# A deformable-patch tokenizer in a vision tower: the four images of a sampling step moved from 32-row bands to 80 adjacent partitions, their places loaded by one transfer

## The reference, cut to what matters

```python
off = conv(x, offset_w, stride 16)            # 2 x 256 offsets (dy, dx) for each of the 800 patches
py  = base_y + ki + dy ;  px = base_x + kj + dx     # 256 places in each patch
sampled = bilinear(x, py, px)                 # zero outside the image
out = einsum('bhwkc,ock->bohw', sampled, Wk)  # 192 x 768, then norm, GELU
```

## Time and profile before

| | us |
|---|---|
| median of 3 runs | 1366.1 |
| lowest, highest | 1360.94, 1372.89 |
| profiled execution, whole run | 1369.17 |
| its span, first to last instruction | 1367.5 |

### The profile page before, as it was taken

The page is one execution under the profiler, slowest core; times in us unless marked ns, Lnnn a source line. Parts: engine busy times, 40 slices in busy tenths (PEclk is TensorE's granted clock), DMA queues, the critical chain, the costliest instruction groups (busy, mean ns, idle before and its releaser), DMA issues. The chain is left out here.

```text
span 1367.5 us, 26288 instructions
## 1 busy us (share of the span) xinstructions
PE 963.0 (70%) x9931; PEld 776.8 (57%) x9931; DVE 675.1 (49%) x1535; ACT 432.3 (32%) x727; POOL 219.7 (16%) x238
## 2 busy tenths in 40 slices
PE   4847778772666559829888547868665999668494
PEld 1337677421333349727778536656534999656473
DVE  2649989624777343164554223645366111146354
ACT  0148888311333212122434312334210121123132
POOL 0143323101000124213111001010002232110100
PEclk9969999985555569966999757958576899859598
DMA  3334444445000257010000060000041798100000
GB/s 119 78 88 130 130 130 131 116 115 139 1 0 0 71 177 202 20 49 2 2 2 2 1 156 2 3 1 2 1 127 34 172 259 194 33 1 3 0 4 19
DMA packets 66324, 92.96 MB, mean 68 GB/s; under 512 B 18164, under 2 KB 53096, under 8 KB 66224
## 3 DMA queue, kind: packets, MB, share of 16 engines
q1 hardware_dynamic: 60720, 85.85, 23.4%
q0 software_dynamic: 5504, 5.70, 2.1%
HBM read 83.93 MB, written 8.12 MB: 67 GB/s over the span
## 5 line engine op out<-in xcount | busy, mean ns | idle before, releaser
L1742 PE MATMUL ps_rows<-stage_strip,stage_hat_y 128*128 128x168 f32 x800 | 134.0, 322 | 47.7 <-ACT stage_hat_y L1709 47.7
L1742 PEld LDWEIGHTS ps_rows<-stage_strip,stage_hat_y 128*128 128x128 f32 x800 | 123.9, 194 | 57.7 <-issue 29.6
L1773 DVE TENSOR_TENSOR stage_product<-ps_rows,stage_hat_x 128x504 f32<-128x504 f32 (+1 forms) x160 | 83.7, 586 | 21.6 <-PE ps_rows L1742 21.3
L1781 DVE TENSOR_REDUCE stage_samples<-stage_product 128x1680 f32 x40 | 76.1, 1903 | 8.5 <-DVE stage_product L1773 7.1
L2537 DVE TENSOR_TENSOR L_ffnhid<-L_ffnact_gate,L_ffnbank_u 128x300 f32<-128x300 f32 x32 | 14.9, 467 | 117.6 <-ACT L_ffnact_gate L2555 117.6
L1724 POOL TENSOR_TENSOR stage_hat_x<-stage_pos_xT,stage_w_window_x 128x280 f32<-128x280 f32 x80 | 53.6, 692 | 113.9 <-DVE stage_product L1773 112.1
L1704 ACT ACTIVATE stage_hat_y<-stage_hat_y,stage_w_minus_row 128x1280 f32<-128x1280 f32 x40 | 54.5, 1362 | 42.1 <-DMA stage_hat_y<-places_y 42.0
L1547 PE MATMUL ps_conv<-stage_w_offset_w,stage_patches 128*100 128x512 f32 x96 | 44.8, 619 | 17.2 <-DMA stage_patches<-in_patchesT 17.2
L1132 PE MATMUL L_attnbank_q<-L_attnhT,L_attnwq 97*128 97x200 f32 x192 | 47.6, 399 | 5.9 <-DVE L_attnqT L1295 5.5
L1709 ACT ACTIVATE stage_hat_y<-stage_hat_y 128x1280 f32<-128x1280 f32 x40 | 50.1, 1254 | 0.0
L1132 PEld LDWEIGHTS L_attnbank_q<-L_attnhT,L_attnwq 97*128 97x128 f32 x192 | 40.2, 230 | 9.1 <-issue 8.3
(11 more groups left out here) (419 smaller groups left out, 2254.9 us busy)
## 6 DMA issues: line engine op xcount, KB each, us to landing
stage_hat_y<-places_y SPq DMA_DIRECT2D x160, 110.0 KB
L_ffn_win<-in_L_ffn_Win SPq DMA_DIRECT2D x10, 1152.0 KB
stage_L_ffn_win<-in_L_ffn_Win SPq DMA_DIRECT2D x6, 1152.0 KB, 9.5
L_ffnranks<-stage_ranks SPq DMA_DIRECT2D x16, 400.0 KB
L_ffn_win<-in_L_ffn_Win SPq DMA_DIRECT2D x8, 768.0 KB
L_ffn_wout<-in_L_ffn_Wout SPq DMA_DIRECT2D x10, 576.0 KB
stage_strip<-in_strips SPq DMA_DIRECT2D x160, 23.5 KB
stage_L_ffn_wout<-in_L_ffn_Wout SPq DMA_DIRECT2D x6, 576.0 KB, 7.0
```

Source lines behind the costliest of these rows:

```text
L1742: mm = nc.tensor.matmul(ps[:, p % 2, h, bank, at * cols:(at + 1) * cols], hat_y[:, p, g, h * P:(h + 1) * P], rhs.rearrange("q j c x -> q ( ...
L1773: last = nc.vector.tensor_tensor(split(product[:, p % 2, h, patches[0] * cols:(patches[-1] + 1) * cols]), split(ps[:, p % 2, h, bank, 0:le ...
L1781: nc.vector.tensor_reduce(into, by_window, AX_X, ALU.add).then_inc(s["summed"], 1)
```

## The change

- `MARGIN` is 2 instead of 3. A window is 20 rows and 12 columns instead of 22 and 14. A strip keeps 84 columns instead of 91.
- The four images of a step lie on the partitions 20j to 20j+19, 80 in all, without gaps. `hat_y` and `strip` have 80 partitions, and `hat_y` isn't cleared any more.
- The places of the four images come in one transfer. Its source is a pattern of 4 images x 20 repeats x 1,280 values, its destination 80 partitions x 1,280. The four strips stay four transfers.
- The ten products of a step fill four banks as 3, 3, 3, 1, and VectorE multiplies in two instructions, one over three banks (1,296 elements) and one over one (144).
- `samples` is laid out by half, channel, token. The reduction writes it with a step from channel to channel, the projection reads 400 neighbouring values, and L1885 puts tokens back in the order of image and column as it writes.

```diff
-MARGIN = 3
+MARGIN = 2
+ROWS_Y = IMG_PER_TILE * WINDOW
+SPAN = PATCH * (GRID - 1) + HALF_COLS + WINDOW_X
+SLOTS = KHALVES * GRID
+PER_BANK = 512 // (IMG_PER_TILE * CHANNELS * WINDOW_X)
...
-        any_far(tw, k, clear=(hat_y, strip))
-        with nc.psum_tensor("ps_rows", [P, 2, KHALVES, 2, 512], F32) as ps, nc.Block() as block:
+        any_far(tw, k, clear=(strip,))
+        with nc.psum_tensor("ps_rows", [P, 2, 4, 512], F32) as ps, nc.Block() as block:
...
+                    version = 0 if kind == NEAR else wy + 1
+                    places = k.rel_d[version].rearrange("(t j h w) c -> t h j (w c)", t=TILES, j=IMG_PER_TILE, h=GRID)[t][ho]
+                    sp.dma_start(hat_y[:, p].rearrange("q w c -> q (w c)"),
+                                 places.unsqueeze(1).to_broadcast([IMG_PER_TILE, WINDOW, GRID * KPOINTS])).then_inc(loads[kind]["places"][p], 16)
                     for j in range(IMG_PER_TILE):
-                        q = slice(QUAD * j, QUAD * j + WINDOW)
-                        version = 0 if kind == NEAR else wy + 1
-                        places = k.rel_d[version].rearrange("(t j h w) c -> t h j (w c)", t=TILES, j=IMG_PER_TILE, h=GRID)[t][ho][j:j + 1, :]
-                        sp.dma_start(hat_y[q, p].rearrange("q w c -> q (w c)"), places.to_broadcast([WINDOW, GRID * KPOINTS])).then_inc(loads[kind]["places"][p], 16)
+                        q = slice(WINDOW * j, WINDOW * (j + 1))
                         if kind == NEAR:
                             sp.dma_start(strip[q, p, j], ins["strips"][ho][t][j]).then_inc(loads[kind]["pixels"][p], 16)
...
                     for h in range(KHALVES):
-                        for bank, patches in enumerate(BANKS):
-                            for at, g in enumerate(patches):
...
+                        for g in range(GRID):
+                            bank, at = divmod(h * GRID + g, PER_BANK)
...
+                            mm = nc.tensor.matmul(ps[:, p % 2, bank, at * cols:(at + 1) * cols], hat_y[:, p, g, h * P:(h + 1) * P], rhs.rearrange("q j c x -> q (j c) x"), start=True, stop=True)
...
+                    full = SLOTS // PER_BANK
+                    for banks, slots in ((slice(0, full), slice(0, full * PER_BANK)), (slice(full, full + 1), slice(full * PER_BANK, SLOTS))):
...
-                    into = k.samples[:, ho * TILES + t, :]
+                    into = k.samples[:, :, :, bass.ds((ho * TILES + t) * IMG_PER_TILE * GRID, IMG_PER_TILE * GRID)]
...
-                                rhs = k.samples[:, half * chunks:(half + 1) * chunks, :].rearrange("q a (h g j c) -> q a j h g c", h=KHALVES, g=GRID, c=CHANNELS)[:, :, :, h, :, c]
+                                rhs = k.samples[:, h, c, half * half_cols:(half + 1) * half_cols]
...
-                    nc.vector.tensor_scalar(normed[:, o, :].rearrange("q (a b) -> q a b", a=2), ps[:, o, :, 0:half_cols], moments[:, o, 0:1], rstd[:, o, :],
+                    nc.vector.tensor_scalar(normed[:, o, :].rearrange("q (a b j w) -> q a b w j", a=2, j=IMG_PER_TILE, w=GRID),
+                                            ps[:, o, :, 0:half_cols].rearrange("q a (b w j) -> q a b w j", j=IMG_PER_TILE, w=GRID), moments[:, o, 0:1], rstd[:, o, :],
...
-        self.samples = tw.sb("samples", [P, GRID * TILES, IMG_PER_TILE * KHALVES * GRID * CHANNELS])
+        self.samples = tw.sb("samples", [P, KHALVES, CHANNELS, IMAGES * TOKENS])
```

More of the change, by code:

```diff
@@ L1632, in sample @@
     cols = IMG_PER_TILE * CHANNELS * WINDOW_X
-    BANKS = (range(0, 3), range(3, GRID))
     B = BUFFERS
@@ L1657, in all_loaded @@
     def all_loaded(eng, kind, what, i, p):
-        eng.wait_ge(loads[kind][what][p], 16 * IMG_PER_TILE // BUFFERS * (i - p + BUFFERS))
+        each = 16 * (IMG_PER_TILE if what == "pixels" else 1)
+        eng.wait_ge(loads[kind][what][p], each // BUFFERS * (i - p + BUFFERS))
     with tw.scratch():
-        hat_y = tw.sb("hat_y", [P, BUFFERS, GRID, KPOINTS])
-        strip = tw.sb("strip", [P, BUFFERS, IMG_PER_TILE, CHANNELS, PADDED])
+        hat_y = tw.sb("hat_y", [ROWS_Y, BUFFERS, GRID, KPOINTS])
+        strip = tw.sb("strip", [ROWS_Y, BUFFERS, IMG_PER_TILE, CHANNELS, SPAN])
         window = strip[:, :, :, :, 0:WINDOW_X]
[L1666 to L1670, removed]
-        any_far(tw, k, clear=(hat_y, strip))
-        with nc.psum_tensor("ps_rows", [P, 2, KHALVES, 2, 512], F32) as ps, nc.Block() as block:
+        hat_x = tw.sb("hat_x", [P, BUFFERS, SLOTS * IMG_PER_TILE, WINDOW_X])
+        product = tw.sb("product", [P, 2, SLOTS * cols])
+        part = tw.sb("part", [P, KHALVES, CHANNELS, GRID * IMG_PER_TILE])
+        moved_places = product[0:TILE_TOKENS].rearrange("q b n -> q (b n)")[:, 0:TILES * KPOINTS].rearrange("q (t n) -> q t n", t=TILES)
+        any_far(tw, k, clear=(strip,))
+        with nc.psum_tensor("ps_rows", [P, 2, 4, 512], F32) as ps, nc.Block() as block:
             @block.sync
@@ L1737, in step @@
                     for h in range(KHALVES):
[L1738 to L1742 removed]
+                        for g in range(GRID):
+                            bank, at = divmod(h * GRID + g, PER_BANK)
+                            left = PATCH * g + HALF_COLS * h
+                            rhs = strip[:, p, :, :, left:left + WINDOW_X] if kind == NEAR else window[:, p]
+                            mm = nc.tensor.matmul(ps[:, p % 2, bank, at * cols:(at + 1) * cols], hat_y[:, p, g, h * P:(h + 1) * P], rhs.rearrange("q j c x -> q (j c) x"), start=True, stop=True)
                     mm.then_inc(s["rows_in_psum"], 1)
@@ new lines, in step @@
+                    for banks, slots in ((slice(0, full), slice(0, full * PER_BANK)), (slice(full, full + 1), slice(full * PER_BANK, SLOTS))):
+                        n_banks, used = banks.stop - banks.start, (slots.stop - slots.start) // (banks.stop - banks.start)
+                        split = lambda x: x.rearrange("q (b w c x) -> q b w c x", b=n_banks, c=CHANNELS, x=WINDOW_X)
+                        weights = hat_x[:, p, slots.start * IMG_PER_TILE:slots.stop * IMG_PER_TILE].rearrange("q (b w) x -> q b w x", b=n_banks).unsqueeze(3)
+                        last = nc.vector.tensor_tensor(split(product[:, p % 2, slots.start * cols:slots.stop * cols]),
+                                                       ps[:, p % 2, banks, 0:used * cols].rearrange("q b (w c x) -> q b w c x", c=CHANNELS, x=WINDOW_X),
+                                                       weights.to_broadcast([P, n_banks, used * IMG_PER_TILE, CHANNELS, WINDOW_X]), ALU.mult)
@@ L1780, in step @@
                     if kind == NEAR:
-                        nc.vector.tensor_reduce(into, by_window, AX_X, ALU.add).then_inc(s["summed"], 1)
+                        nc.vector.tensor_reduce(into.rearrange("q h c w -> q h w c"), by_window, AX_X, ALU.add).then_inc(s["summed"], 1)
                     else:
-                        nc.vector.tensor_reduce(part[:], by_window, AX_X, ALU.add).then_inc(s["summed"], 1)
+                        nc.vector.tensor_reduce(part[:].rearrange("q h c w -> q h w c"), by_window, AX_X, ALU.add).then_inc(s["summed"], 1)
@@ L2905, in layout @@
     rows = padded.transpose(0, 2, 1, 3).reshape(TILES, IMG_PER_TILE, PADDED, CHANNELS, PADDED)
-    o["strips"] = np.stack([rows[:, :, PATCH * g:PATCH * g + WINDOW] for g in range(GRID)])
+    o["strips"] = np.stack([rows[:, :, PATCH * g:PATCH * g + WINDOW, :, :SPAN] for g in range(GRID)])
     at = lambda i, size: slice(MARGIN + size * i, MARGIN + size * (i + 1))
```

11 lines of the change are left out of this document (5 added, 6 removed).

## The result

| | before | after |
|---|---|---|
| median of 20 runs, us | 1366.8 | 1374.0 |
| profiled span, us | 1367.5 | 1373.6 |
| ratio of the undisturbed runs, 95% interval | | 1.0062 (1.0039 to 1.0085) |

Single executions can be disturbed (one of the kernel before took 2562 us), so all ratios here are taken over the undisturbed runs, and are not quotients of the medians.

A forecast was written before the change was run, and what follows sets the result against it. VectorE bounded the sampling stage before, four DMA engines at 4.8 us a step would after; block ahead -3.6, stage +20.3, projection -15.0 give +1.7 us, put on the median 1368 us, range 1343 to 1397.

The forecast's parts named there:

- The transfer on four engines: Sampling stage: the one transfer of places runs on 4 engines, each with 20 packets of 5,120 bytes.
- Its pace: Sampling stage: the four DMA engines need 4.8 us a step, bounds 4.16 to 6.4 us.
- TensorE: Sampling stage: a step's passes fall from 3.25 to 2.85 us at full clock, at most 5.7 at 1.2 GHz.
- What would show it: Signs: about 44 small packets a step, DMA share near 0.35, ScalarE waiting over 1 us, 4.8 us periods, L1860 at 0.34.
- The first landing: Start of the sampling stage: 6.0 us from SP's first issue to ScalarE's start, against 2.28 after the fourth issue before.
- The block ahead: Ahead of the sampling stage: GpSimd's first clearing goes and the second shrinks, gain 3.6 us.
- The projection: Behind the stage: 48 passes reading neighbouring columns fall from 33.28 to 18.0 us, gain 15.0, bounds nothing to 16.8.
- The scaling: L1885 after the projection: writing with a step costs 0 to +2 us, taken as 0.
- (b): Rival, sampling stage: four engines, but fast ones, period 4.16 to 4.4 us, 1343 to 1352 us; chance 0.15.
- (a): Rival, sampling stage: places spread over 16 engines, VectorE bounds, stage 154.5 us, whole 1319 us; chance 0.13.
- (c): Rival, sampling stage: four engines, slow, period above 5.1 us, 1395 us at 5.5, 1430 at 6.4; chance 0.18.
- (d): Rival, projection: it gains nothing, since TensorE waits for something else there, +15, 1383 us; chance 0.06.

The follow-up runs named there:

- the experiment with ten engines: The changed kernel with partitions ordered by row and then image, so the one transfer of places counts 20 repeats outermost, 80 rows: 1380.7 us, ratio 1.012.
- the first experiment: The changed kernel with hat_y and strip on 128 partitions, cleared once, products over all 128 rows, places still in one transfer: 1354.7 us, ratio 0.992.
- the 80-row kernel with six issues: The kernel of four places transfers, two strips transfers and early clearing, with buffers of 80 instead of 128 partitions: 1368.4 us, ratio 0.999.
- its 128-row twin: Against the changed kernel: 128 rows, four transfers of places, strips in two transfers with stored zeros, buffers cleared while first weights load: 1312.9 us, ratio 0.960.

## Why the prediction was right in its number and wrong in its cause

- **The transfer on four engines: right.** Packets under 512 bytes are 1,455 in 90 to 250 us, for 33 to 34 steps 44 each (4 + 4 x 10), and the DMA share is 0.35, as foretold. The Trainium skill (DMA: Bandwidth & Descriptors, "Why a DMA increments its semaphore by 16 and not by 1") gives this count, and the experiment with ten engines agrees with it at 50 small packets a step.
- **Its pace: mis-sized.** The term "I take 4.8 us" measured 4.3, near the lower bound of 4.16. Both prices in it were too high together: the data alone, at the 24.4 GB/s that it took from the earlier trace rows, would need 110.5 / 24.4 = 4.5 us, and the completions another 0.45. The runs don't tell how the 4.3 us divide between them.
- **TensorE: the step that failed.** The prediction let the passes "have 144 instead of 168 columns, 3.25 becomes 2.85 us at the full clock", and of the fall to 1.2 GHz it said "buffers take up single ones; I add nothing". It treated the lower clock as an accident of single steps. In the kernel after it holds in every step, 20 x 0.24 = 4.80 us, and buffers can't hide a rate. The step from 128 to 80 rows stood in the change, and the prediction gave it no price at all. That the mistaken 4.8 and the true 4.80 are equal is chance: with the DMA's 4.3 alone the same sum would have given 39 x 0.5 = 20 us less, 1348 us, and the first experiment, which has just that, ran at 1354.7 with some 3 us more of clearing. The 5.7 us that it named as the most for a step at the low clock was too high as well (measured 4.80, and 2.7 at the full clock).
- **The signs of being right all came true and didn't tell the causes apart.** Packets, DMA share, ScalarE's wait, the period, VectorE's lengths and L1860 (0.336 us a pass) are as listed under "What would show it". None of them looks at TensorE's clock or asks who waits for whom. ScalarE's wait for places is there in the 80-row kernel with six issues too (40.5 us in 32 steps) and all but gone in its 128-row twin with the same transfers (0.7 us in 31): with slow products the buffers come free late, and so the transfers start late.
- **The first landing: too early.** Predicted 6.0 us from SP's first issue to ScalarE's start, measured 7.7 (74.51 to 82.21). With the first products at 1.2 GHz (4.80 for 2.85 us) and 39 periods of 4.82 for 4.8, this makes 1.7 + 1.95 + 0.8 = 4.5 of the 4.9 us by which the stage exceeds its 203.0.
- **The block ahead: right**, 3.6 us, to within 0.1.
- **The projection: right**, 14.4 us for 15.0 (33.28 - 18.0, by its own terms, is 15.3); eight passes, not five, ran at the lower clock.
- **The scaling: 1.1 us**, inside the stated 0 to +2 but taken as 0. The reduction's scattered write costs nothing, as taken.
- **VectorE's step of 3.53 us: right**, and to be seen once all covers are gone (128 rows, places on ten engines, five or six issues).
- **The rivals.** (b), four fast engines, was right on the DMA (4.3) and wrong on the time, because TensorE took over. (a) names the time that the stage could have had. (c) and (d) didn't happen.

## What to carry to other kernels

When two resources can each explain a period, make each free by itself; in the kernel after, both seemed to need 4.8 us and only one was the bound. Products on fewer partitions are not free: look at the granted clock of the stretch after such an edit, and if it has fallen while TensorE is never idle, padding the operands with rows of zeros may be the cheapest cure. Issue costs and engine counts are separate prices of a merged transfer: here one or two transfers of strips served equally well, four kept SP at 4 us a step, and one transfer of places sat on four engines. Before crediting an edit with a gain, check that the kernel just before it, looked at in the same window, hadn't got it already.

## What the runs showed of the hardware that was not expected

- **The clock and the rows of a product.** In this stage float32 products of 80 rows kept TensorE busy for 190 us, and the granted clock stayed at 0.50 (so in four kernels with different transfers, three without a gap and one with gaps of 2.5 us in 80). With 128 rows, 48 of them zeros, it was 0.97 to 1.00 in the first experiment, 0.84 to 1.00 in the others, and with 96 rows 0.71 to 0.83. The Trainium skill (TensorE: Matmul & The Clock Gate, "What's actually happening") says that the clock follows how busy the engine has been; here the busier engine had the lower clock, so busy time alone doesn't decide. Nor do rows alone. In an expert layer of the kernel before, products of 96 rows and 100 columns fill about 5.5 of every 7.5 us (those between have 100 and 128 rows). There TensorE is busy all the time too, and the clock is full:

```profile
1090.00:1100.00 10.00, 10.00 (x87) 9.96 (x86) 0.94 (x2) 1.78 (x5) 4.30 (x3) 1.00 1.04 248
```

Thirty us earlier in the same layer (1060 to 1070) it was busy 10.00 of 10 us at 0.50, and between 620 and 630 us, where nearly all products have 96 or 97 rows and most of the time goes to those of 200 and 384 columns, 9.88 of 10 us at 0.50. What the chip counts isn't known from these runs, and these stretches show that the three row counts of this stage are no table for other products.
- **SP's price for a transfer** depends on its pattern: four strips to 20 neighbouring partitions each take 1.72 us (0.47 to 0.48 from one to the next), four to 20 partitions four apart 3.55; the record of the transfer of 4 images x 20 repeats alone is 0.67 to 0.86 us long, against 0.29 for a single image's.
- **Columns 12 bytes apart** cost TensorE twice as much as neighbouring ones at the full clock (0.69 against 0.336 us a pass) and nothing more at the lower one (0.69 against 0.667): 33.28 against 18.64 us for the same 48 passes.
- **GpSimd's clearing holds up some of VectorE's small instructions**: the three `tensor_scalar` of the block ahead, the first of them 7.46 us in place of 0.17 (the latter with the clearing done early). The two reductions just before them took 0.17 and 0.16 us beside the same clearing.
